# A decoder layer on one core: orders written out at both ends, a few operations on other engines, once-only work placed among the batches

## The reference

```python
q, k, v = x @ Wq.T + bq, x @ Wk.T + bk, x @ Wv.T + bv        # 16 heads of 16
scores  = einsum(q, k) / 4 + pos_bias[:, i - j + 255]
x = layernorm(x + softmax(scores) @ v @ Wo.T + bo)
# q = x, k = v = ctx: 4 heads of 64, gates from [x, ctx, ctx]
ig, fg = gates;  cs = cumsum(log_sigmoid(fg))
log_D  = cs_i - cs_j + ig_j  (j <= i);  m = max_j log_D
C = (q k / 8) * exp(log_D - m)
h = C / (max(|sum C|, exp(-m)) + 1e-6) @ v
x = layernorm(x + per_head_norm(h) * outnorm_scale)
# bitlinear: rows of x rounded to 8 bits, weights to -1, 0, 1
x = layernorm(x + bitlinear(silu(bitlinear(x, w_gate)) * bitlinear(x, w_up), w_down))
```

## Time and profile before

| | us |
|---|---|
| median of 3 runs | 768.72 |
| lowest, highest | 763.31, 770.01 |
| the profiled execution | 766.44 |
| its span, first to last instruction | 764.6 |
| transfers of the whole run | 68.32 MB |

### The profile page before, as it was taken

How to read it: one execution, slowest core, us unless ns; L and a number is a source line. 1 busy time by engine, 2 the same in 40 slices (tenths; PEclk the granted TensorE clock), 3 DMA queues, 4 the chain that set the end, 5 groups by cost and what they waited for, 6 DMA issues and landing times.

```text
span 764.6 us, 17069 instructions
## 1 busy us (share of the span) xinstructions
PE 640.8 (84%) x4882; PEld 476.4 (62%) x4912; DVE 617.4 (81%) x2261; ACT 597.5 (78%) x1253; POOL 483.2 (63%) x833
## 2 busy tenths in 40 slices
PE   4367997999999999999999999989999989785542
PEld 3345776667676758686868676867676757452311
DVE  2755464899999999999999999988999999875752
ACT  0415795999999998989898999988999989875421
POOL 2415654667777868787778777776777765535332
PEclk8587998999999999999999999999999999897855
DMA  8887624154445545454545453635353542120201
GB/s 266 156 143 111 97 60 74 23 114 65 123 74 112 83 113 84 111 84 112 84 111 84 109 87 89 95 85 101 70 117 60 108 59 72 42 56 15 69 15 41
DMA packets 96966, 68.32 MB, mean 89 GB/s; under 512 B 40229, under 2 KB 96618, under 8 KB 96874
## 3 DMA queue, kind: packets, MB, share of 16 engines
q1 hardware_dynamic: 96874, 67.23, 44.7%
HBM read 29.39 MB, written 4.26 MB: 44 GB/s over the span
## 4 chain that ended last, share of the span: by engine, by line
PE 28%; DMA 23%; ACT 13%; SPq 10%; DVE 10%; issue 10%; POOL 6%; POOLq 0%; ACTq 0%; DVEq 0%
DMA mb<-mrows 13%; DMA th<-hq 7%; SPq L299 6%; PE pT L615 3%; PE pO L632 3%; ACT L997 2%; PE pA L751 2%; ACT h L1124 2%; SPq L337 2%; DVE mm L1568 2%; PE pB L739 2%; DMA ks<-parts 2%; PE pB L764 1%; PE pB L761 1%; PE pS L599 1%
## 5 line engine op out<-in xcount | busy, mean ns | idle before, releaser
L1292 DVE CUSTOM_DVE_ANT_0 sc<-pS,bias 128x256 f32<-128x256 f32 x512 | 201.4, 416 | 28.0 <-PE pS L599 26.8
L947 ACT ACTIVATE pr<-pT 128x512 f32<-128x512 f32 x256 | 154.5, 608 | 22.0 <-PE pT L615 21.4
L615 PE MATMUL pT<-ident,sc 128*128 128x128 f32 x1024 | 153.1, 277 | 5.1 <-POOL sc L437 3.2
L437 POOL TENSOR_SCALAR sc<-sc,mx 128x256 f32<-128x256 f32 x256 | 123.3, 493 | 23.3 <-DVE mx L1292 20.8
L615 PEld LDWEIGHTS pT<-ident,sc 128*128 128x128 f32 x1024 | 119.6, 142 | 28.1 <-issue 17.1
L935 ACT ACTIVATE sc<-sc,mx 128x256 f32<-128x256 f32 x256 | 130.2, 516 | 3.0 <-DVE mx L1292 3.0
L599 PE MATMUL pS<-ks,qs 96*128 96x256 bf16 x512 | 93.8, 274 | 9.1 <-DVE mx L1292 6.5
L489 POOL TENSOR_SCALAR_AFFINE_SELECT mb<-mb 128x256 f32<-128x256 f32 x64 | 26.3, 411 | 80.2 <-ACT mb L974 79.2
L632 PE MATMUL pO<-pr,va 128*32 128x256 f32 x1024 | 70.2, 393 | 0.5 <-ACT pr L947 0.5
L599 PEld LDWEIGHTS pS<-ks,qs 96*128 96x128 bf16 x512 | 47.9, 98 | 34.0 <-DVE mx L1292 17.0
L449 POOL TENSOR_SCALAR hq<-h 128x512 bf16<-128x512 f32 x64 | 38.7, 620 | 32.0 <-ACT h L1124 31.8
(11 more groups left out here) (223 smaller groups left out, 1736.3 us busy)
## 6 DMA issues: line engine op xcount, KB each, us to landing
qs<-parts SPq DMA_DIRECT2D x96, 128.0 KB, 4.7
ks<-parts SPq DMA_DIRECT2D x96, 128.0 KB, 4.5
mb<-mrows SPq DMA_DIRECT2D x16, 512.0 KB, 7.5
xin<-in_x SPq DMA_DIRECT2D x16, 256.0 KB, 2.8
bias<-in_L_attn_pos_bias SPq DMA_DIRECT2D x4, 1024.0 KB, 20.8
xb<-in_x SPq DMA_DIRECT2D x16, 256.0 KB, 3.0
cx<-in_ctx SPq DMA_DIRECT2D x32, 128.0 KB, 2.1
out<-hq SPq DMA_DIRECT2D x16, 256.0 KB, 3.2
```

Of the source, the lines that this page charges most:

```text
L437: pool.tensor_scalar(sc[:, s % RING, 1, :], sc[:, s % RING, 1, :], -1.0, mx[:, s % RING, 1:2], ALU.mult, ALU.add).then_inc(neg_g.sem, 1)
L615: ins = pe.transpose(bank[:, kt * S + t * P:kt * S + t * P + P], sc[:, s % RING, t, kt * P:kt * P + P], ident[:])
L947: act.activation(flat(pr[:, s % RING, :, :]), pT[s % 2][:, :], ACT.Exp, scale=-1.0)\
L1292: dve.tensor_tensor_reduce(out=sc[:, s % RING, t, :], in0=pS[s % 2][:, t * S:t * S + S], in1=bias[:, t, s, ::-1], scale=1.0, scalar=LOW, o ...
```

## The change

Ten edits, some of which the diff shows in part only:

1. The iterations are replaced by `opening()`, `body(b)` for b from 4 to 11, and `closing()`. The first and the last are lists of single steps with fixed batch numbers, one list for each engine. `body` has another order on every engine.
2. What is done once is cut into steps (`weight_turned`, `weight_copied`, `weight_load`, `weight_sums`, `weight_mean`, `weight_inverse`, `weight_round`, `weight_signs`, `weight_turn`, `weight_scales`, `gate_weights`) that stand in `opening()` among the heads of batches 0 and 1.
3. The inner weights are loaded one after the other into h, in pieces of 128 columns, and transposed by one DMA each (2048 columns) instead of on TensorE.
4. The bias is held as 384 columns for a head, of which each half reads 256, instead of two times 256. It is loaded in four transfers of four heads.
5. bqk and the three broadcast rows come straight from DRAM. `apart` is gone.
6. k of batch 0 is split on VectorE (`k_split`).
7. Heads 2, 7 and 12 have both halves negated on GpSimd.
8. `quantised_rows` and `input_rows` move from VectorE to GpSimd. `quantised_rows` is now x times 1 plus -MAGIC.
9. The four gate products go side by side into four 32-column strips of one bank (`gate_parts`), ScalarE copies them (`gate_copy`), and one product with a matrix of zeros and ones (`fold`) adds them (`gate_sums`).
10. A bank is leased to whichever use stands third after the last one in the written order, instead of by the table `uses`.

```diff
+POOL_HEADS = (2, 7, 12)
-        bias = sb("bias", [P, TT, NH, S])
+        bias = sb("bias", [P, NH, S + P])
-        gate_w = sb("gate_w", [P, 6, 64 + XH])
+        gate_w = sb("gate_w", [P, 6, 32])
+        fold = sb("fold", [P, 64 + XH])
...
         def lease(eng, name, batch):
+            if len(leases) >= len(shared):
+                other, n = leases[-len(shared)]
+                signal, k = freed[other]
+                eng.wait_ge(signal.sem, signal.at(n, k))
+            banks[name, batch] = shared[len(leases) % len(shared)]
+            leases.append((name, batch))
+            return banks[name, batch]
...
+            def gate_parts(c):
+                for j in range(4):
+                    rows = cxT if j < KT else x1T
+                    ins = pe.matmul(bank[32 * j:32 * j + 32, 0:S], gate_w[:, 2 + j if j < KT else j - KT, :],
+                                    rows[:, j % KT, :], start=True, stop=True)
+            def gate_sums(c):
+                pe.wait_ge(gp_sb.sem, gp_sb.at(c, 1))
+                pe.matmul(bank[0:64 + XH, 0:S], fold[:, :], gt[:, :], start=True, stop=True).then_inc(gt_ps.sem, 1)
...
+            def load_bias(g):
+                src = bass.AP(tensor=pos_bias.tensor, offset=g * GH * 1023, ap=[[1, P], [1023, GH], [1, S + P]])
+                sp.dma_start(bias[:, g * GH:g * GH + GH, :], src).then_inc(d_bias[g].sem, 16)
+            def weight_load(i):
+                if i:
+                    sp.wait_ge(wt_v.sem, 2 * i)
+                dst = stage.rearrange("p (a b c) -> p a b c", b=FT if i < 2 else KT, c=P)
+                src = (w_gate, w_up, w_down)[i].rearrange("(b p) (a c) -> a p b c", p=P, c=P)
+                for a in range(KT if i < 2 else FT):
+                    sp.dma_start(dst[:, a, :, :], src[a]).then_inc(d_wf.sem, 16)
+            def weight_turn(i):
+                sp.wait_ge(wt_v.sem, 2 * i + 2)
+                dst = (wg, wu, wd)[i][:, :, :].rearrange("p a b -> p (a b)").rearrange("p (g r) -> p g r", r=P)
+                sp.dma_start_transpose(dst, tern[i]).then_inc(d_wt[i].sem, 16)
```

The opening on SyncE:

```diff
+            def opening():
+                load_bias(2)
+                load_bias(3)
+                load_gates(0)
+                weight_load(0)
+                load_stack(0, 0, 0)
+                load_stack(0, 0, 1)
+                load_x(2, 0)
+                weight_load(1)
+                load_stack(1, 1, 0)
+                load_x(3, 1)
+                load_stack(1, 1, 1)
+                load_residual(0)
+                weight_turn(0)
+                weight_load(2)
+                weight_turn(1)
+                load_stack(2, 0, 0)
```

The period on SyncE:

```diff
             def body(b, par=None):
-                turn_inner(d, 1)
-                save_max(f)
+                store(d)
+                load_residual(c)
                 load_x(n2, par)
-                load_residual(c)
-                spread_max(f)
+                turn_inner(e, 0)
+                load_ctx(c)
+                turn_inner(e, 1)
                 load_stack(n, 1 - par, 0)
-                store(d)
-                load_ctx(c)
-                turn_inner(e, 0)
                 load_stack(n, 1 - par, 1)
+                save_max(c)
+                spread_max(c)
```

The negation on GpSimd:

```diff
             def negated(b, s):
-                pool.tensor_scalar(sc[:, s % RING, 1, :], sc[:, s % RING, 1, :], -1.0, mx[:, s % RING, 1:2],
-                                   ALU.mult, ALU.add).then_inc(neg_g.sem, 1)
+                for t in range(TT) if s in POOL_HEADS else (1,):
+                    ins = pool.tensor_scalar(sc[:, s % RING, t, :], sc[:, s % RING, t, :], -1.0, mx[:, s % RING, t:t + 1],
+                                             ALU.mult, ALU.add)
+                ins.then_inc(neg_g.sem, 1)
```

The opening on VectorE, and the loop that every engine ends with:

```diff
+            def opening():
+                weight_copied(0)
...
+                weight_sums(0)
+                v_copy(0, 0)
+                weight_inverse(0)
+                weight_signs(0)
+                biased(0, 0, 0)
...
+            opening()
+            for b in range(FIRST, LAST):
+                body(b)
+            closing()
```

More of the change, by code:

```diff
@@ L224, in lease @@
         def lease(eng, name, batch):
-            n = names.index(name)
-            it = batch + uses[n][1]
-            for back in range(1, 2 * len(uses)):
-                i, m = (it, n - back) if back <= n else (it - 1, n - back + len(uses))
-                if m < 0:
-                    break
-                other, behind, freed, k = uses[m]
-                if bank_of(other) is bank_of(name) and live(i - behind):
-                    wait(eng, freed, i - behind, k)
-                    break
@@ L608, in turned @@
                 bank = pT[s % 2]
-                pe.wait_ge(neg_a.sem, lin + 1)
+                act_heads = s + 1 - sum(h <= s for h in POOL_HEADS)
+                if s not in POOL_HEADS:
+                    pe.wait_ge(neg_a.sem, neg_a.at(b, act_heads))
                 pe.wait_ge(neg_g.sem, lin + 1)
@@ L1202, in _ @@
[L1202 to L1208 removed]
+                mem_late(c, 1)
+                negated(b, 15)
+                mem_weights(c, 1)
+                mem_late(c, 2)
+                exponentials(b, 14)
+                mem_weights(c, 2)
+                heads_copy(b, 2)
@@ L1211, in _ @@
+            act.wait_ge(g_set.sem, G_ALL)
+            opening()
+            for b in range(FIRST, LAST):
+                body(b)
+            closing()
         @block.vector
@@ L1280, in _, with scaled_bias, gate_weights @@
-            assert done[0] == V_ALL
+                    step(dve.tensor_copy((wvT, woT)[k // KT - 2][:, k % KT, :], pb[k % 4][:, 0:D]))
+            def scaled_bias(i):
+                dve.wait_ge(d_qk.sem, 16 * 2)
+                step(dve.tensor_scalar(bqk[:, 0, :], bqk[:, 0, :], DH ** -0.5, None, ALU.mult))
+            def gate_weights(c):
+                dve.wait_ge(d_gates.sem, 16 * 4)
+                dve.wait_ge(g_set.sem, G_ALL)
+                for part in range(2):
+                    dve.tensor_reduce(fold[:, 64 * part:64 * part + XH],
+                                      ident[:, :].rearrange("p (j c) -> p c j", j=4)[:, XH * part:XH * part + XH, :],
+                                      AX.X, ALU.add).then_inc(gw_set.sem, 1)
+                dve.tensor_tensor(gate_w[:, 2:4, :], gate_w[:, 2:4, :], gate_w[:, 4:6, :], ALU.add).then_inc(gw_set.sem, 1)
```

3281 lines of the change are left out of this document (2706 added, 575 removed).

## The result

The changed kernel takes 747.37 us in the median of four runs (745.26 to 749.83), where the kernel before took 769.15 beside it. The ratio is 0.973, with an interval from 0.968 to 0.979. The profiled execution took 745.26 us, with a span of 743.3. So the span fell by 21.3 us, not by the 47 of the forecast.

The account below looks back on a forecast made before the run. Transfers were taken to hold the opening, three engines at once the middle, a chain through every engine the tail. Gains of 12 + 6 + 7 + 13 + 9 = 47 us off a 764.6 span gave 719 in all, range 690 to 746.

Parts of the forecast that it names:

- part E: From batch 12's running maximum to the end: 167.5 us for 176.7, 9 gained, bounds 15 and 2.
- D: Ten steady periods: each falls from 39.8 to 38.5 us, 13 gained, bounds 25 gained and 5 lost.
- B: From first scores to first running maximum: 47 us for 53.2, 6 gained, bounds 15 gained and 4 lost.
- C: From the first running maximum to batch 2's: 75 us for 82.0 by a written order, 7 gained, bounds 12 and 1.
- A: Up to the first scores: 43 us for 54.9 through fewer bytes loaded, 12 gained, bounds 6 and 20.
- Rival 1: Steady period stays at 39.8 us, bound by the loop through two transfers; 736 us in all, chance 0.18.
- the work cut of 1.0 to 1.2 us should come out of the period: Steady period: less work on three full engines shortens it, with 0.1 to 0.2 of waits, from 39.8 to 38.5 us.
- bias priced by its pieces: Opening up to the first scores: the upper bound, 20 us gained, with half as many bias pieces.
- no longer waits for all constants before batch 1's projections: First scores to first maximum: TensorE does about the same work with less waiting; 47 us taken for 53.2.
- The danger named for this part: First scores to first maximum: three DMA weight transposes stand in SyncE's queue ahead of batches 2 and 3's stacks.
- rival 4: Steady period: GpSimd becomes the bound, its period 42.2 us with its waits kept; 785 us in all, chance 0.08.
- Rival 3: Steady period: GpSimd's added 2.6 us hold VectorE up as long, period 41.4; 762 us in all, chance 0.05.

Follow-up runs that it names:

- a1: The changed kernel with the bias in two copies of 256 columns, eight transfers instead of four: 759.49 us, one run.
- e2: The changed kernel with the opening's steps for iterations 1 to 3 put into the order of the period: 753.80 us.
- e1: The changed kernel with the written-out closing replaced by the same steps in the order of the period: 743.94 us.
- h1: The changed kernel with iterations 2, 3 and 12 to 14 in the period's order, the other ends as written: 741.40 us.
- a2: The changed kernel with the first stack and first seven heads ahead of gate loads, weight steps and batch 1's projections: 766.21 us.
- u_gates: The changed kernel with the four gate products in one accumulation again, without copy and fold: 756.43 us, one run.
- t1: The changed kernel with the second half of the sum left out of each gate product, output altered: 747.29 us, one run.
- t2: The changed kernel with half of the columns left out of each first gated product, output altered: 741.41 us, one run.
- m_more_heads: The changed kernel with heads 5 and 10 also negated on GpSimd: 749.07 us, one run.
- u_rows: The changed kernel with quantised_rows and input_rows on VectorE again: 748.47 us, one run.

## Why the prediction was wrong

**The level.** 719 was forecast, with a range that ended at 746; 747.37 is just past it. The direction was right, and of the 26 us missed, 14.7 are part E, 8 are D, 5 each B and C, less 6.5 of A. Rival 1 (the period stays at 39.8, 736) came nearest: the period shrank by 0.9 instead of 1.3, but rival 1 kept the gains of the ends, and those are what failed. By size the steps that failed are E's "38.5 + 35 + 35 and 59" (it measured 182.4 for 167.5), then D's "the work cut of 1.0 to 1.2 us should come out of the period", then the times of B and C; each is taken up below.

**Part A, the way right and the gain undersized.** The stretch was bound by transfers, and the byte count pointed the right way. The step that failed is "of the 2.7 MB saved only 1.0 is bias, the dearer kind". That one megabyte alone brought 12 us (a1, one run), the whole of the term that I took, and the upper bound of 20, "bias priced by its pieces", was the better value. The bias loads are shorter in sum, as foretold: the earlier trace rows has 14.34 us of issue, after has 3.60.

**Part B.** The step "no longer waits for all constants before batch 1's projections" did not pay. The weight work did fit beside the heads: VectorE has 37.7 and ScalarE 38.5 of 51.7 us. But TensorE is the fullest engine, and its work hardly shrank. It had 46.3 us of the 53.15 before:

```profile
54.90:108.05 53.15, 46.32 (x340) 35.58 (x341) 28.59 (x141) 36.75 (x79) 31.41 (x53) 0.90 0.52 75
```

and has 44.7 of 51.7 after, 7 us of idle time in both. The 47 us would have left it 2.3. And room on an engine is not room on the path: two of the weight steps that "fit" stand in the chain that ended last (start, us, what):

```profile
52.25 1.99 ACT h L2088
...
70.20 2.10 ACT h L2088
```

The danger named for this part, the three weight transposes in SyncE's queue, shows with 11.5 us of issue, among the stacks; what it costs was not measured:

```profile
52.61 4.44 SPq L1210 DMA_TRANSPOSE wg<-hq  x1
61.43 2.59 SPq L1210 DMA_TRANSPOSE wu<-th  x1
64.12 4.47 SPq L1225 DMA_DIRECT2D qs<-parts  x6
...
90.76 4.47 SPq L1210 DMA_TRANSPOSE wd<-hq  x1
```

**Parts C and E, a premise without a row.** "With an order written for them I take 75" and "three periods, with the last two short of a next batch" both took an order made for a place to be better there. No row bore that out. E's sum was 38.5 + 35 + 35 and 59, and it measured 40.4, 42.0, 38.6 and 61.5; the kernel before had 39.8, 37.2, 39.5 and 60.2, so the 35 for batch 14 was the term furthest off. The premise was true for the first iterations (12.7 us, e2) and for batch 15 (e1), and false for iterations 3, 12 and 13, where the period's own order gives 38.9 for 41.5, 40.4 and 40.4 (and in 14, 40.4 for 41.9). Of E's 5.7 us lost, 1.2 are only the mark, against batch 13's first head: from there to the end it is 219.8 us, 215.3 before. 1.5 of that goes with the generic order (h1, 218.3), and the kernel with TensorE's idle time filled has another 3.2 less. Two heavy waits of the tail are in both kernels, as "the tail has little to give" said. (Before, TensorE waits 7.52 us for the rows and 7.08 for th there.) TensorE in after, in order of time:

```profile
683.08 0.58 PE L274 MATMUL pB<-ident_b,xq 128*128 128x128 bf16 x4 [7.42 <-POOL xq L1463]
...
716.50 0.59 PE L274 MATMUL pA<-ident_b,xq 128*128 128x128 bf16 x4 [9.47 <-POOL xq L1463]
...
732.63 1.86 PE L456 MATMUL pA<-wd,th 128*128 128x256 bf16 x8 [7.37 <-DMA th<-hq]
```

Why the tail is 61.5 and not 60.2 stays open; with the same closing it is 61.5 to 63.9 in e2, a2 and a1, so the difference is less than what comes and goes by itself.

**Part D, the terms right and the sum wrong.** The busy times of a period came as worked out: VectorE 35.8 (forecast 35.9), ScalarE 35.6 (35.5), GpSimd 32.2 (32.7); seven `quantised_rows` took 645 ns each (0.62) and six `input_rows` 726 (0.5), in groups by line from 248 to 482 us. VectorE's match is in part luck: its scan takes 0.5 us more than before (1.55 for 1.04), which the forecast had at nothing, and smaller steps make up for it.

```profile
L1463 POOL TENSOR_SCALAR xq<-att 128x512 bf16<-128x512 f32 x7 | 4.5, 645 | 0.0
L1513 POOL TENSOR_TENSOR am<-gt,cs 4x256 f32<-4x256 f32 x6 | 4.4, 726 | 17.1 <-DVE cs L3059 17.1
```

TensorE's term was oversized: in the chain of after the strips take 0.57 and the fold 0.64 (start, us, what), for 0.45 and 0.43, so 0.5 us are saved and not 0.84; 0.4 of the period came out of it (u_gates). Even by the prediction's own picture the engine that loses least would have set the gain, and TensorE's 0.84 is less than "1.0 to 1.2".

```profile
317.38 0.57 PE pB L470 x8
...
318.55 0.64 PE pA L480 x2
```

The step that failed is "the work cut of 1.0 to 1.2 us should come out of the period", with its picture of three engines that bound at once. An engine that is 95% busy need not be the bound. Less work on one of them changed nothing (t1, t2; m_more_heads with more on VectorE), while 1.5 us put back on ScalarE came out in full. And two of the moves in the old order were worth nothing. What does set 38.9 us stays open. The second row above shows one place where time is now spent waiting: GpSimd's `input_rows` waits 2.85 us in each period for `forget_sums`, and its queue stands.

**The rivals.** Rival 1 came near in its number, but not by its mechanism: between 209 and 521 us no engine of the changed kernel shows a wait for a transfer, of mb or of th. GpSimd did not become the bound (rival 4): its idle time fell from 9.5 us of 39.6 to 6.7 of 38.9, as the forecast wanted. Rival 3, exclusion, did not decide either, but its instance is real. The scan L3067, with GpSimd's rows and negations beside it (VectorE and GpSimd in the changed kernel, in order of time):

```profile
325.77 0.65 POOL L1463 TENSOR_SCALAR xq<-att 128x512 bf16<-128x512 f32 x1
325.86 1.55 DVE L3067 TENSOR_TENSOR_SCAN mm<-am 4x256 f32<-4x256 f32 x1
326.41 1.28 POOL L1453 TENSOR_SCALAR sc<-sc,mx 128x256 f32<-128x256 f32 x2
```

and the same scan with both rows on VectorE (u_rows), where GpSimd is idle at that moment:

```profile
327.82 0.67 DVE L3065 TENSOR_TENSOR_SCAN mm<-am 4x256 f32<-4x256 f32 x1
```

1.55 us for 0.67, and two negations in 1.28 for 0.99 (L1453 takes 497 ns in the mean). In u_rows the two rows themselves take VectorE 0.41 us each, so moving them took 0.82 us off VectorE, and 0.88 came back in the scan: against u_rows the move is worth nothing there. Against the kernel before, whose rows took 0.61 and 0.41 and whose scan took 1.04, it is 1.02 off and 0.5 back. The Trainium skill (SBUF — State Buffer, Who interferes with whom) names a VectorE instruction with two SBUF inputs as one that contends with a GpSimd instruction that reads SBUF; the scan reads am twice, and these rows agree.

## What to carry to other kernels

Busy shares tell how much work there is, not what a microsecond less is worth: take work away from one engine and look at the period before a sum is made of it. An order and the division of the work fit each other; in the old order two of the same moves were worth nothing, and an order with the work put back was worse than the old one. Where a written-out opening or closing meets a loop, compare it iteration by iteration with the loop's own order and keep the shorter of the two. And before a stretch is dated by a step, see whether the change has moved that step.

## What the runs showed of the hardware

- The bias in eight transfers with rows of 256 columns, for four with rows of 384, is 1.05 MB more and put the first scores off by 11.9 us in one run, where 8.0 MB had moved in 36.4.
- A scan of 4x256 on VectorE takes 0.67 us with GpSimd idle and 1.55 beside GpSimd's quantised rows and negations; `forget_sums` (L3059), of the same size, during which GpSimd waits, stays at 0.68.
- TensorE's granted clock followed its idle time: 0.66 in the last 62.4 us, and 0.81 with products that nobody reads in the gaps.
